# Decoder layer with a mixture of experts: dense experts replaced by picked tokens sorted into 53 expert tiles

## The reference, cut to what matters

```python
def _L0_ffn_ref(x, router_w, router_b, temperature, wg, wp, wo):   # E, FF, K = 8, 256, 2
    scores = (jnp.einsum('btd,ed->bte', x, router_w) + router_b) / temp
    gates = _sinkhorn(scores)                       # 3 rounds over experts and over tokens
    topk_vals, topk_idx = jax.lax.top_k(gates, K)
    topk_gates = topk_vals / (jnp.sum(topk_vals, axis=-1, keepdims=True) + 1e-08)
    g = jax.nn.relu(jnp.einsum('btd,edf->btef', x, wg))
    p = jnp.einsum('btd,edf->btef', x, wp)
    all_out = jnp.einsum('btef,efd->bted', g * p, wo)
    gathered = jnp.take_along_axis(all_out, topk_idx[..., None], axis=2)
    return x + jnp.sum(gathered * topk_gates[..., None], axis=2)
```

## Time and profile before

| | us |
|---|---|
| median of three runs | 419.12 (418.45 to 419.6) |
| the profiled execution, its own time | 422.17 |
| span of the profiled execution | 420.4 |
| PE busy | 356.0 (85%) |
| DVE busy | 262.3 (62%) |
| ACT busy | 146.0 (35%) |
| POOL busy | 144.6 (34%) |
| DMA | 23.84 MB, 22216 packets |

### The profile page before, as it was taken

How to read it: one execution, slowest core, us unless ns; L and a number is a source line. 1 busy time by engine, 2 the same in 40 slices (tenths; PEclk the granted TensorE clock), 3 DMA queues, 4 the chain that set the end, 5 groups by cost and what they waited for, 6 DMA issues and landing times.

```text
span 420.4 us, 5562 instructions
## 1 busy us (share of the span) xinstructions
PE 356.0 (85%) x1896; PEld 235.4 (56%) x1909; DVE 262.3 (62%) x628; ACT 146.0 (35%) x276; POOL 144.6 (34%) x150
## 2 busy tenths in 40 slices
PE   1546678579987999779996899999999899999995
PEld 1333345343464535445454543687788688888883
DVE  6595376882297924971249831576779766666662
ACT  2503404816634265005531146222221323223221
POOL 7331213562012130011003020356354565666563
PEclk9985676979999999999798799999899999999998
DMA  4203650331004210153001200321100242220000
GB/s 109 68 1 81 174 192 1 94 72 38 2 0 115 54 37 0 40 122 93 0 2 50 94 16 2 125 51 50 50 27 25 68 123 69 82 64 26 27 0 25
DMA packets 22216, 23.84 MB, mean 57 GB/s; under 512 B 5117, under 2 KB 17341, under 8 KB 21973
## 3 DMA queue, kind: packets, MB, share of 16 engines
q1 hardware_dynamic: 21805, 23.29, 20.2%
q10 hardware_dynamic: 384, 0.20, 0.2%
HBM read 20.11 MB, written 3.18 MB: 55 GB/s over the span
## 4 chain that ended last, share of the span: by engine, by line
PE 60%; DVE 21%; ACT 5%; issue 4%; DMA 4%; POOL 4%; ACTq 1%; SPq 0%; POOLq 0%; DVEq 0%
DVE nmax_mask L984 6%; PE pC L1337 4%; PE pS L1322 4%; PE pC L1334 4%; PE pS L1319 3%; PE pS L268 3%; PE pS L270 3%; PE pS L269 3%; PE pG L1116 2%; PE pS L1286 2%; PE pA L268 2%; PE pS L1289 2%; PE pB L268 2%; PE pB L270 2%; PE pB L269 2%
## 5 line engine op out<-in xcount | busy, mean ns | idle before, releaser
L586 POOL TENSOR_TENSOR xi_lo<-xi_f,xi_hi 128x512 fp32r<-128x512 f32 x43 | 55.8, 1299 | 53.4 <-ACT xi_hi L739 53.2
L984 DVE TENSOR_REDUCE nmax_mask<-pS 128x3 f32<-128x462 f32 (+1 forms) x96 | 52.7, 578 | 18.1 <-PE pS L1289 17.2
L707 ACT ACTIVATE prob<-pS 128x512 f32<-128x512 f32 x80 | 42.4, 600 | 33.4 <-PE pS L1322 30.3
L739 ACT CAST xi_hi<-xi_f 128x512 fp32r<-128x512 f32 x43 | 26.7, 621 | 65.8 <-DVE xi_f L1039 65.8
L1039 DVE TENSOR_TENSOR xi_f<-sig,pS 128x512 f32<-128x512 f32 x64 | 44.0, 688 | 3.9 <-PE pS L270 0.6
L1286 PE MATMUL pS<-k_stack,q_stack 72*128 72x154 bf16 x256 | 36.7, 249 | 3.2 <-DMA q_stack<-q_scr 3.1
L586 POOL TENSOR_TENSOR act_lo<-xi_f,act_hi 128x512 fp32r<-128x512 f32 x21 | 27.5, 1310 | 27.1 <-ACT act_hi L739 27.1
L1289 PE MATMUL pS<-mbias,ident_bf 128*128 128x462 bf16 (+1 forms) x96 | 36.3, 378 | 0.0
L1286 PEld LDWEIGHTS pS<-k_stack,q_stack 72*128 72x128 bf16 x256 | 22.0, 107 | 12.1 <-issue 7.1
L1283 PE MATMUL pS<-mbiasT,ident_bf 128*128 128x128 bf16 x72 | 17.5, 243 | 11.7 <-DVE nmax_mask L984 11.4
L739 ACT CAST act_hi<-xi_f 128x512 fp32r<-128x512 f32 x21 | 13.0, 620 | 41.0 <-DVE xi_f L1039 41.0
(11 more groups left out here) (332 smaller groups left out, 846.3 us busy)
## 6 DMA issues: line engine op xcount, KB each, us to landing
prob<-w_scr SPq DMA_DIRECT2D x16, 256.0 KB, 3.3
q_stack<-q_scr SPq DMA_DIRECT2D x9, 384.0 KB
q_scr<-q_parts SPq DMA_DIRECT2D x12, 128.0 KB, 2.4
k_stack<-k_scr SPq DMA_DIRECT2D x36, 40.0 KB
res<-in_x_dram SPq DMA_DIRECT2D x4, 256.0 KB, 4.6
prob<-in_L_ffn_wg_dram SPq DMA_DIRECT2D x1, 1024.0 KB, 5.9
prob<-in_L_ffn_wp_dram SPq DMA_DIRECT2D x1, 1024.0 KB, 8.3
ctx_in<-in_L_ffn_wo_dram SPq DMA_DIRECT2D x4, 256.0 KB, 3.1
```

What stands on the lines that cost most here:

```text
L586: pool.tensor_tensor(hid_lo[u % NHID], hid[:, u % 2, :], f32(hid_hi[u % NHID]), ALU.subtract).then_inc(s_hidlo, 1)
L707: act.activation(prob[:, (NSB * b + n) % NBUF, :], score_bank(b, NSA + n)[:, :], ACT.Exp).then_inc(s_exp, 1)
L739: act.copy(hid_hi[u % NHID], hid[:, u % 2, :]).then_inc(s_hidhi, 1)
L984: dve.tensor_reduce(nmax[:, qt, hs[0]:hs[-1] + 1], score_bank(b, n)[:, 0:len(hs) * KEYS].rearrange("p (h k) -> p h k", k=KEYS), AX.X, ALU. ...
```

## The change

The tokens' picks are sorted by expert, so that each expert works only on the tokens that picked it.

- **Groups and tiles.** Three routing groups: batches 0 and 1, batch 2, batch 3. Each group's picks (2 for a token) are placed in rows sorted by expert, each expert padded to a multiple of 128 rows. The number of tiles is fixed at its maximum: 23, 15 and 15, in all 53 tiles of 128 rows.
- **Placing.** New DVE and PE steps "rank" and "place" work out each pick's row. Group 0's are at slots 13, 25, 25, 26 and 30 of batch 3.
- **Sorting.** POOL writes normalised tokens to DRAM with indirect DMAs: 8 for each batch, 128 rows of 516 bytes each (128 features and the row's return address). The first batch of group 0 is scattered at slot 26 of batch 3, the second at slot 34. The DRAM rows are first filled with blanks, 14 SP DMAs in batch 1 (slots 28 to 41).
- **A tile.** SP loads up to four tiles in one DMA; PE transposes them (4 transposes of 128x128), ACT and DVE make halves. PE reads the tile's expert number into a register and addresses the weights with it. Three matmuls of 512 columns give gate and up together. ACT takes the relu (128x256), DVE multiplies (128x256), PE transposes the product (two 128x128), ACT copies two tiles at a time (128x512), and PE forms the down product as two plain fp32 matmuls of 128 columns a tile, not split in halves. ACT copies two tiles' outputs (128x256).
- **Back.** For groups 0 and 1, SP writes outputs in pairs of tiles to DRAM, and POOL gathers them by token, 8 indirect DMAs for a batch. For the last group, POOL scatters each tile by token with one indirect DMA (15 in all), then SP reads batch 3's two halves back. DVE adds with the gate as scalar: 8 instructions of 128x128 for a batch, then SP stores.
- **Gone.** The gate rows through DRAM, the splitting of the down weights, the 64 units.
- **Moved.** Logits are made for each batch in "post" at slot 35. Group 1's router starts in batch 3 (slots 36 to 46), its rest and group 2's router are spread over tiles 0 to 26. "residual" on POOL now also copies the normalised tokens and writes row numbers.

```diff
+    GRP = [(0, 2), (2, 1), (3, 1)]
+    NTILES = [(PICKS * nb * S + E * (P - 1)) // P for _, nb in GRP]
+    CH = 4
...
+        NSLOT = 3
+        NHID = 4
+        NY = 8
+        NWRITE = 4
...
+        ROUTER_AT = ([36, 37, 38, 38, 39, 40, 41, 42, 43, 44, 45, 46],
+                     [0, 1, 2, 3, 4, 5, 7, 9, 11, 13, 25, 25, 26, 30, 26, 34])
+        ROUTER1_AT = [36, 37, 38, 38, 39, 40, 41, 42, 43, 44, 45, 46]
+        TAIL_AT = [0, 0, 1, 2, 3, 3, 3, 5, 6, 6, 7, 8, 8]
+        REST1_AT = [0, 1, 1, 2, 3, 3, 4, 5, 6, 7, 8, 9, 10, 12, 9]
+        ROUTER2_AT = [9, 10, 10, 11, 11, 12, 12, 13, 13, 14, 15, 15, 16, 17, 17, 18, 19, 19, 20, 20, 21, 22, 23, 23, 24,
+                      26, 24]
+        GATHER_AT = [27, 28, 43]
+        ADD_AT = [39, 45, 52]
+        STORE_AT = [42, 48]
+        AHEAD, LOAD_AHEAD = 3, 6
...
+        STEPS += [("load_rows", c, 0) for c in early]
+        STEPS += last_group(NB - 1)[1:]
+        STEPS += [("sort_T", 0, 0), ("sort_T", 1, 0)]
+        for j in range(2 * NPAIR + 4):
+            if j + LOAD_AHEAD in first_up:
+                STEPS.append(("load_rows", first_up[j + LOAD_AHEAD], 0))
+            if j >= 2 and j + AHEAD in first_up and first_up[j + AHEAD] > 1:
+                STEPS.append(("sort_T", first_up[j + AHEAD], 0))
+            if j < NT:
+                STEPS.append(("up", j, 0))
+                STEPS += left[j]
+            if j % 2 == 1:
+                k = j // 2 - 1
+                if 0 <= k - 1 < NPAIR:
+                    STEPS.append(("down", k - 1, 0))
+                if 0 <= k < NPAIR:
+                    STEPS.append(("hid_T", k, 0))
+        STEPS += [("store", NB - 2, 0), ("combine", NB - 1, 0), ("store", NB - 1, 0)]
...
+                elif step == "load_rows":
+
+                    g, t0, nt = CHUNKS[b]
+                    sp.wait_ge(s_in[g], 16 * PICKS * T * GRP[g][1])
...
+                elif step == "scatter":
+
+                    first, nb = GRP[b]
+                    if b == 0:
+                        pool.wait_ge(s_filled, 16 * NC)
+                    pool.wait_ge(s_pos, PLACE_STEPS * b + PLACED)
+                    pool.wait_ge(s_extb, (PICKS + 1) * (first + nb))
+                    for t in range(T):
+                        for k in range(PICKS):
+                            blk = t * nb + n
+                            pool.indirect_dma_start(
+                                out=sort_scr[b][:, :],
+                                out_offset=bass.IndirectOffsetOnAxis(ap=pick_row[k][b][:, blk:blk + 1], axis=0),
+                                in_=ext_of(first + n, k)[:, t, :], in_offset=None,
+                                bounds_check=NTILES[b] * P - 1, oob_is_err=False).then_inc(s_in[b], 16)
...
+            def up(j, e):
+                c = CHUNK_OF[j]
+                col = (j - CHUNKS[c][1]) * P
+                x_hi, x_lo = (half[:, c % 2, col:col + P] for half in sortT)
+                w_hi, w_lo = (half[:, :, :, :].rearrange("p e w f -> p (e w f)")[:, bass.ds(e * (2 * FF), 2 * FF)]
+                              for half in wgp)
+                three_pass(pe, pUp[j % 2][:, :], x_hi, x_lo, w_hi, w_lo).then_inc(s_up, 1)
+
+            def down(j, e):
+                for h in range(HF):
+                    col = (j % 2) * FF + h * P
+                    last = pe.matmul(pO[:, (j % 2) * D:(j % 2 + 1) * D], hidT[:, (j // 2) % 2, col:col + P],
+                                     wo_sb[:, bass.ds(e * (HF * D) + h * D, D)], start=(j % 2 == 0 and h == 0),
+                                     stop=(h == HF - 1), skip_group_check=True)
+                last.then_inc(s_down, 1)
...
+                    experts[b] = pe.value_load(tile_expert[0:1, b:b + 1], min_val=0, max_val=E - 1)
+                    pe.wait_ge(s_sortlo, CHUNK_OF[b] + 1)
+                    if b >= 2:
+                        pe.wait_ge(s_hid, b - 1)
+                    up(b, experts[b])
```

More of the change, by code:

```diff
@@ L258, in score_bank, with pair, leaving, landed @@
             return pS[((NSA + NSB) * b + k) % len(pS)]
-        def tokens_view(ps):
-            return ps[:, 0:T * GB * E].rearrange("p (t b e) -> p t b e", t=T, b=GB)
+        def pair(k):
+            return list(range(2 * k, min(2 * k + 2, NT)))
+        def leaving(k):
+            tiles = pair(k)
+            groups = [CHUNKS[CHUNK_OF[j]][0] for j in tiles]
+            if len(tiles) == 2 and groups[0] == groups[1] != SCATTERED:
+                return [(groups[0], tiles[0] - TILE0[groups[0]], 0, 2)]
+            return [(g, j - TILE0[g], i, 1) for i, (g, j) in enumerate(zip(groups, tiles))]
+        def landed(k, i):
+            return 16 * sum(len(leaving(j)) for j in range(k + 1) if j % NWRITE == i and 2 * j < WRITTEN)
         def f32(ap):
@@ L342, in router @@
                 steps += [("row_norm", grp, it), ("col_sum", grp, it), ("col_norm", grp, it)]
-            return steps + [("gates", grp, 0), ("gates", grp, 1), ("gates", grp, 2), ("gates_T", grp, 0)]
+            return steps + [("gates", grp, 0), ("gates", grp, 1), ("gates", grp, 2), ("rank", grp, 0),
+                            ("place", grp, 0), ("place", grp, 1), ("place", grp, 2), ("place", grp, 3)] + [
+                ("scatter", grp, i) for i in range(GRP[grp][1])]
         def post(b):
@@ L386, in build_decoder @@
                 place(mix_in(b + 2) + mix_out(b + 2), FIRST_MIX_AT if b == 0 else MIX_AT)
+            if b == 1:
+                place([("fill_rows", 0, c) for c in range(NC)], FILL_AT)
+                slots[0].append(("sort_consts", 0, 0))
             if b == NB - 2:
@@ L389, in build_decoder @@
             elif b == NB - 1:
-                place([("load_wo", 0, i) for i in range(WO_STEPS)], WO_AT[0])
-                place([("split_wo", 0, i) for i in range(WO_STEPS)], WO_AT[1])
+                place([("load_wo", 0, 0)], [0])
                 place(router(0)[len(ROUTER_AT[0]):], ROUTER_AT[1])
+                place(router(1)[:len(ROUTER1_AT)], ROUTER1_AT)
             for g in range(G - 1):
@@ L413, in build_decoder @@
-        STEPS += [("out_T", NB - 1, 0)]
+        left = [[] for _ in range(NT)]
+        for steps, at in ((post(NB - 1), TAIL_AT), (router(1)[len(ROUTER1_AT):], REST1_AT), (router(2), ROUTER2_AT),
+                          ([("gather", b, 0) for b in range(NB - 1)], GATHER_AT),
+                          ([("combine", b, 0) for b in range(NB - 1)], ADD_AT),
+                          ([("store", b, 0) for b in range(NB - 2)], STORE_AT)):
+            for step, j in zip(steps, at, strict=True):
+                left[j].append(step)
@@ L1395, in _ @@
                     for t in range(T):
-                        last = pe.matmul(pSink[b][:, 2 * P:2 * P + GB * E], all_ones[:, :],
-                                         route["gate"][:, b, t, :, :].rearrange("p b e -> p (b e)"), start=(t == 0),
-                                         stop=(t == T - 1), skip_group_check=True)
+                        last = pe.matmul(pSink[b][:, 2 * P:2 * P + rows], all_ones[:, :],
+                                         route["gate"][b][:, t * GRP[b][1]:(t + 1) * GRP[b][1], :].rearrange(
+                                             "p b e -> p (b e)"), start=(t == 0), stop=(t == T - 1),
+                                         skip_group_check=True)
```

708 lines of the change are left out of this document (432 added, 276 removed).

## The result

The changed kernel took 445.4 us, median of four runs (441.3 to 454.2), the kernel before 418.8 in the same session: a ratio of 1.058, interval 1.051 to 1.065. The forecast was 397 with a range up to 418, so it is wrong in sign and size.

What follows compares the result with a forecast made beforehand. PE was taken to bound the last phase (143.7 of 147.2 us busy). First tile at 275.2, tiles 106.6 and tail 16.7 gave a span of 398.5 us against 420.4, so a median of 397.2, range 371 to 418.

Steps and rivals of the forecast that it cites:

- Tiles instead of units: Last phase, the main saving: 1.46 us of PE work a tile, 77.4 us for 53 tiles, where 64 units took 132.5.
- Waits between PE's instructions: Tile stage: PE's register read before each tile costs 0.2 us, 10.6 us in all, within 0 to 0.60 a tile.
- Interleaved PE work: Tile stage: column sums, batch 3's short post-work matmuls, rank and maxima add 9 us on PE.
- The clock: Tile stage: PE's granted clock taken as 0.9 because of short matmuls, 9.6 us more; bounds 1.00 and 0.84.
- The start: Before the tiles: placing, 16 scatters, landing and first load put the first tile at 275.2, 10 us after the first unit.
- p: POOL's time for one indirect DMA, shown by no row: taken as 1.1 us, bounds 0.60 and 2.2.
- The tail: After the last tile: POOL ends 6.3 us after PE's last matmul, then 10.4 us; 16.7 us against 8.2.
- At 2 us a tile both have room: Groups 1 and 2, placed at tiles 8 and 22, scattered in 8.8 us each, are ready before tiles 17 and 32.
- the rivals: Three alternatives to the forecast: POOL's DMAs bound both ends (chance 0.10), register read exposed (0.12), everything clean (0.23).
- POOL's indirect DMAs bound both ends: Rival for start and tail: span 355.6 + 39p, slower from p = 1.66; median 428 at 1.9, 440 at 2.2; chance 0.10.

Runs made afterwards that it cites:

- a0_same: The changed kernel without an edit, run again on another chip: 0.998 (0.995 to 1.002) of the kernel before.
- c1_router_one: Changed kernel with group ranks and the third router's column maximum one tile later, no scatter moved: 410.7 us, 0.981 (0.975 to 0.988) of the kernel before.
- c1_again: The kernel of c1_router_one, run again on another chip: 409.8 us, 0.975 (0.971 to 0.979) of the kernel before.
- b2_busy: Changed kernel with 10 and 12 filler matmuls of 512 columns ahead of two PE waits in the third group's router: 417.6 us.
- b1_router_later: Changed kernel with ranks, places and scatters of groups two and three and the third router 2 to 5 tiles later: 1.011 (1.008 to 1.015) of before.
- a0_third: The changed kernel without an edit, a third repeat, on a chip of the lower level: 0.990 (0.986 to 0.995) of the kernel before.
- the doses: Changed kernel with 8 gathers added (452.9 us, 1.078 of before), or with the 16 gathers of batches 0 and 1 left out (434.1 us, 1.025).
- a0_fourth: The changed kernel without an edit, a fourth repeat, on a chip of the upper level: 446.6 us, 1.054 (1.049 to 1.060) of the kernel before.

## Why the prediction was wrong, step by step

- **Tiles instead of units: right.** 1.46 us of PE work and 0.2 for the read, 1.66 a tile at full clock; 1.69 at a clock of 1.00 in tiles 30 to 49 (33.85 / 20; 1.65 in a0_same). The 53 tiles are 89.6 us against 88.0.
- **Waits between PE's instructions: nearly right.** 0.11 to 0.14 us a tile for 0.2. The figure of some 600 ns in the Trainium skill (DMA: Bandwidth & Descriptors, "Latency and other measured facts") is twice the 0.30 us that the queue shows, and over half of that is hidden.
- **Interleaved PE work: here a term was missing.** I counted the router's PE work (9 us) and not that PE waits for DVE's part of it: 2.9, 2.7, 2.2, 1.4 and 1.5 us, 10.7 in all. The tile stage beyond the bare tiles is 118.4 - 89.6 = 28.8 us; my sum had 9 + 9.6 = 18.6. c1_router_one shortens the waits for rank and column maximum and with them the stretches at the low clock, and its stage of 108.9 us is near the forecast's 106.6.
- **The clock: right on the mean.** 0.89 for 0.9. What it follows was not the share of short matmuls, as I had argued: with the same matmuls it is 0.96 in c1_again, and with a tile's own share of short ones it is 1.00 in tiles 30 to 49. The low stretches lie behind the waits, and in b2_busy filling a wait took one of them away. So the right mean came from a wrong reason, and that is luck.
- **The start: right at the lower level,** 276.2 for 275.2. p is 1.28 for 1.1, some 2.9 us more over 16, so other terms were too large by 1.9; 1.3 of it is that POOL's first scatter starts at 245.5 where I had 246.8.
- **The tail: the mechanism right, p mis-sized.** Batch 2's gathers start at 376.3, 2.1 us into tile 43, and the queue of 23 ends at 405.9, 11.3 us after PE's last matmul. Mine was 6.3; 23 times 0.18 is 4.1 of the 5.0. The rest of the tail is 9.8 us for 10.4.
- **"At 2 us a tile both have room": just so.** In the changed kernel PE waits 1.4 us for rows in the tile stage. There is little to spare: b1_router_later moved the third group's scatter by five tiles and PE stood 8.3 us.

At the lower level this gives the whole difference: 1.0 + 11.8 + 4.4 = 17.2 us of span, and so a kernel that is no slower than before but hardly faster.

The sign of the result is another matter: **the rivals had it wrong in form.** The rival "POOL's indirect DMAs bound both ends" was to decide from p = 1.66. p is 1.27 also in the result's execution, so it did not happen. Its reason was the right one all the same, 71 operations that the kernel before doesn't have and that no row priced. What they cost in the result was PE's time, about 1 us each in tiles 30 to 39, and not POOL's. **The step that failed is that the sum has no term for this:** I priced an indirect DMA only as p in POOL's own queue and put its cost to the other engines at nothing, without a reason. In the result's execution the tile stage takes 149.3 us for my 106.6, and PE is idle in it for 38.4 us, against 118.4 and 16.0 in a0_third. That this comes from POOL's DMAs rests on two things: the doses, which were tried on the chip of a0_fourth, and the result's own trace, in which the ten tiles take the same 31.60 us and PE's late events stand at POOL's bursts. Why one chip does this and another doesn't stays open.

## What to carry to other kernels

An operation that no trace shows needs two bounds: what it takes on its own queue, and what it may do to the others; and a kernel that leans on it should be timed on more than one chip before its gain is believed. When serial work (a router, a placing) is interleaved with a PE stream, place each PE step after the slot in which its input is ready: one tile later was worth 1.7% against the changed kernel on the same chip, up to five tiles later cost 1.8%. Count what stands in one engine's queue from a group's birth to its last use, since a queue without a pause passes every delay of its first element to the end.

## What the runs showed of the hardware

- One indirect DMA of 128 rows occupies POOL for 0.97 to 1.00 us and the next follows 0.30 us later. That holds at both levels, and it is the same for scatter and gather; from issue to landing a median of 2.1 to 2.6 us in a0_third.
- The same kernel has two levels 6% apart on different chips, 0.99 and 1.05 of a kernel without indirect DMAs that doesn't change. On the slow chip ten tiles take 17.4, 31.6 and 41.65 us with 0, 16 and 24 gathers among them, and 33 to 40 of PE's 414 to 421 matched semaphore events come over 0.5 us after their records, all at POOL's indirect DMAs; at the lower level none does.
- A register read from SBUF takes 0.30 us of PE's queue and costs 0.11 to 0.14 us of a tile of 1.69.
- In a0_third the granted clock was 0.50 in 297 to 307, behind a wait of 2.9 us, with PE busy all the time, and 1.00 in tiles 30 to 49, where no wait is over 0.6 us.
